# First layer of a DLRM tower as three fp32r passes on high and low halves

## The reference

```python
def _cin_layer(X0, Xi, W, b):
    Wr = W.reshape(H, F0_, Fi)
    return jnp.einsum('hjk,bjd,bkd->bhd', Wr, X0, Xi) + b[None, :, None]
e = jnp.stack([tbl_0[ids[:, 0]], ..., tbl_38[ids[:, 38]]], axis=1)   # (512, 39, 16)
Xi = e
for W, b in ((W0, b0), (W1, b1), (W2, b2)):                          # H = 128 each
    Xi = _cin_layer(e, Xi, W, b); res.append(Xi.sum(axis=2))
h = jnp.concatenate(res + [dense_ctx], axis=1)                       # (512, 400)
h = relu(h @ W_top1 + b_top1); h = relu(h @ W_top2 + b_top2); y = h @ W_top3
```

## Time and profile before

| | |
|---|---|
| median of 3 runs | 696.32 us (695.70 to 696.78) |
| the profiled execution | 697.1 us, its span 695.2 us |
| mean granted TensorE clock | 0.993 |
| TensorE busy | 651.2 us, 94% of the span |
| VectorE busy | 566.9 us, 82% |
| GpSimd busy | 444.2 us, 64% |
| ScalarE busy | 410.4 us, 59% |

### The profile page before, as it was taken

How to read it: one execution, slowest core, us unless ns; L and a number is a source line. 1 busy time by engine, 2 the same in 40 slices (tenths; PEclk the granted TensorE clock), 3 DMA queues, 4 the chain that set the end, 5 groups by cost and what they waited for, 6 DMA issues and landing times.

```text
span 695.2 us, 10601 instructions
## 1 busy us (share of the span) xinstructions
PE 651.2 (94%) x2856; PEld 495.7 (71%) x2856; DVE 566.9 (82%) x1495; ACT 410.4 (59%) x1369; POOL 444.2 (64%) x372
## 2 busy tenths in 40 slices
...
GB/s 214 49 128 232 151 60 122 6 124 6 124 7 105 24 3 88 43 64 68 58 75 42 83 7 37 95 28 103 18 114 17 99 16 18 111 1 6 0 2 1
DMA packets 39055, 44.33 MB, mean 64 GB/s; under 512 B 17427, under 2 KB 22253, under 8 KB 38867
## 3 DMA queue, kind: packets, MB, share of 16 engines
...
...
## 4 chain that ended last, share of the span: by engine, by line
PE 88%; POOL 4%; DVE 3%; DMA 2%; issue 2%; SPq 1%; ACT 1%; POOLq 0%; DVEq 0%
PE p_u L541 20%; PE p_u L542 20%; PE p_u L543 20%; PE p_x L518 13%; PE p_tower L560 5%; PE p_g L551 5%; POOL emb L257 3%; DVE parts L449 1%; DVE x2t L457 1%; PE p_tower L587 1%; PE p_tower L573 1%; DMA emb<-table_in,idx_all 1%; PE p_tower L572 1%; PE p_tower L579 1%; PE p_x L508 1%
## 5 line engine op out<-in xcount | busy, mean ns | idle before, releaser
L331 ACT ACTIVATE prod<-p_u,x0t 128x128 f32<-128x128 f32 x1024 | 290.9, 369 | 140.4 <-PE p_u L543 140.1
L449 DVE SCALAR_TENSOR_TENSOR parts<-p_u,x0t,parts 128x128 f32<-128x128 f32 x1024 | 283.7, 343 | 50.4 <-PE p_u L543 50.3
L541 PE MATMUL p_u<-w1h,x1h 128*128 128x512 f32 (+1 forms) x640 | 303.9, 475 | 4.1 <-DVE x1l L426 2.3
L542 PE MATMUL p_u<-w1l,x1h 128*128 128x512 f32 (+1 forms) x640 | 250.4, 391 | 0.0
L543 PE MATMUL p_u<-w1h,x1l 128*128 128x512 f32 (+1 forms) x640 | 250.2, 391 | 0.0
L273 POOL TENSOR_TENSOR parts<-parts,prod 128x512 f32<-128x512 f32 x128 | 173.1, 1353 | 77.6 <-ACT prod L331 66.3
L257 POOL DMA_INDIRECT emb<-table_in,idx_all x176 | 181.3, 1030 | 51.2 <-issue 47.8
L541 PEld LDWEIGHTS p_u<-w1h,x1h 128*128 128x128 f32 x640 | 120.9, 189 | 52.6 <-issue 20.4
L268 POOL TENSOR_TENSOR parts<-prod 128x512 f32<-128x512 f32 x64 | 89.6, 1400 | 99.6 <-ACT prod L331 99.3
L542 PEld LDWEIGHTS p_u<-w1l,x1h 128*128 128x128 f32 x640 | 121.5, 190 | 42.8 <-issue 20.2
L543 PEld LDWEIGHTS p_u<-w1h,x1l 128*128 128x128 f32 x640 | 120.7, 189 | 25.8
...
## 6 DMA issues: line engine op xcount, KB each, us to landing
...
bd<-x0t SPq DMA_DIRECT2D x128, 10.0 KB, 2.1
```

Source lines behind the costliest of these rows:

```text
L331: last = nc.scalar.activation(dst[:, i * H:(i + 1) * H], u[:, i * H:(i + 1) * H], ACT.Copy, scale=x0t[:, par, t, j:j + 1])
L449: nc.vector.scalar_tensor_tensor(out=chain[:, p, i, :], in0=u[:, i * H:(i + 1) * H], scalar=x0t[:, par, t, j:j + 1], in1=add, op0=ALU.mult ...
L541: nc.tensor.matmul(u, xh, wh, start=True, stop=False)
L542: nc.tensor.matmul(u, xh, wl, start=False, stop=False)
```

## The change

**What it does.** The first layer is computed as the second one already is. w0 and each z0 are split into a high half, rounded to fp32r, and the low half that is left. Instead of one float32 matmul a group, TensorE does three fp32r ones: high w by high z, low w by high z, high w by low z.

(In the diff, the hunks are in this order: constants, wait helper, GpSimd, ScalarE, VectorE, TensorE.) ScalarE makes each high half z0h one slot after the product. The low half z0l = z0 - z0h is made by VectorE two slots after the product for k = 0, 2, 4, 6, and by GpSimd for k = 1, 3, 5, in the tiles 0, 1 and 2 of the macro, between its first and second add. S_ADD moves one slot later, and with it x1f, x1h and x1l. The product no longer waits for TensorE to be done with the ring's place but for the low half made from it; the new rings z0h and z0l are the ones that wait for TensorE. w0 is split once at the start.

```diff
-S_ADD = [s + 6 for s in S_PAIR]
+S_HIGH = [s + 1 for s in S_PAIR]
+S_LOW = [s + 2 for s in S_PAIR]
+S_ADD = [s + 7 for s in S_PAIR]
+LOW_POOL = (1, 3, 5)
+LOW_DVE = (0, 2, 4, 6)
...
+        def wait_low(engine, M, k):
+            if M == 0:
+                engine.wait_ge(z0l_dve, k + 1)
+            elif k in LOW_DVE:
+                engine.wait_ge(z0l_dve, GROUPS + len(LOW_DVE) * (M - 1) + LOW_DVE.index(k) + 1)
+            else:
+                engine.wait_ge(z0l_pool, len(LOW_POOL) * (M - 1) + LOW_POOL.index(k) + 1)
...
+            def low_half(M, k):
+                rows = GROUP_ROWS[k]
+                pool.wait_ge(z0h_made, GROUPS * M + k + 1)
+                need(pool, l0_added, GROUPS * M + max(k - Z_RING + 1, 0))
+                nc.gpsimd.tensor_tensor(out=z0l[0:rows, k % Z_RING, :], in0=z0[0:rows, k % Z_RING, :],
+                                 in1=z0h[0:rows, k % Z_RING, :].bitcast(FP32), op=ALU.subtract).then_inc(z0l_pool, 1)
...
                     for i in (2, 3):
+                        if i == 2 and t < len(LOW_POOL) and (has_next or m < MACROS - 1):
+                            low_half(n * MACROS + m + 1, LOW_POOL[t])
...
+            def make_z0h(M, k):
+                rows = GROUP_ROWS[k]
+                act.wait_ge(z0_made, GROUPS * M + k + 1)
+                need(act, l0_added, GROUPS * M + max(k - Z_RING + 1, 0))
+                nc.scalar.activation(z0h[0:rows, k % Z_RING, :], z0[0:rows, k % Z_RING, :], ACT.Copy).then_inc(z0h_made, 1)
...
                 dve.wait_ge(b_in[k], 16 * (M + 1))
-                need(dve, l0_added, GROUPS * M + max(k - Z_RING + 1, 0))
+                if k >= Z_RING:
+                    wait_low(dve, M, k - Z_RING)
+                elif M > 0:
+                    wait_low(dve, M - 1, max(range(k, GROUPS, Z_RING)))
...
+                        for k in LOW_DVE:
+                            if prepares and s == S_LOW[k]:
+                                low_half(M + 1, k)
...
             for k in range(GROUPS):
                 product(0, 0, 0, k)
+                if k > 0:
+                    low_half(0, k - 1)
+            low_half(0, GROUPS - 1)
...
-                pe.wait_ge(z0_made, GROUPS * M + k + 1)
-                nc.tensor.matmul(p_x1[:], w0[0:rows, k * H:(k + 1) * H], z0[0:rows, k % Z_RING, :],
-                                 start=(k == 0), stop=(k == GROUPS - 1)).then_inc(l0_added, 1)
+                pe.wait_ge(z0h_made, GROUPS * M + k + 1)
+                wh, wl = w0h[0:rows, k * H:(k + 1) * H], w0l[0:rows, k * H:(k + 1) * H]
+                zh, zl = z0h[0:rows, k % Z_RING, :], z0l[0:rows, k % Z_RING, :]
+                nc.tensor.matmul(p_x1[:], wh, zh, start=(k == 0), stop=False)
+                nc.tensor.matmul(p_x1[:], wl, zh, start=False, stop=False)
+                wait_low(pe, M, k)
+                nc.tensor.matmul(p_x1[:], wh, zl, start=False, stop=(k == GROUPS - 1)).then_inc(l0_added, 1)
```

More of the change, by code:

```diff
@@ L87, in build @@
         w0 = sb("w0", [ROWS, GROUPS * H])
+        w0h = sb("w0h", [ROWS, GROUPS * H], FP32R)
+        w0l = sb("w0l", [ROWS, GROUPS * H], FP32R)
         w1h = sb("w1h", [H, F * H], FP32R)
@@ L104, in build @@
         z0 = sb("z0", [ROWS, Z_RING, COLS])
+        z0h = sb("z0h", [ROWS, Z_RING, COLS], FP32R)
+        z0l = sb("z0l", [ROWS, Z_RING, COLS], FP32R)
         x1f = sb("x1f", [H, COLS])
@@ L144, in build @@
         w0_summed = sem("w0_summed")
+        w0h_made = sem("w0h_made")
+        w0l_made = sem("w0l_made")
         w1h_made = sem("w1h_made")
@@ L154, in build @@
         z0_made = sem("z0_made")
+        z0h_made = sem("z0h_made")
+        z0l_dve = sem("z0l_dve")
+        z0l_pool = sem("z0l_pool")
         l0_added = sem("l0_added")
@@ L370, in body @@
                             evac_x0t(M + 1, n * (MACROS // 2) + (m + 1) // 2, (m + 1) % 2)
+                        for k in range(GROUPS):
+                            if prepares and s == S_HIGH[k]:
+                                make_z0h(M + 1, k)
                         if prepares and s == S_ADD[-1]:
@@ L399, in _ @@
             evac_x0t(0, 0, 0)
+            act.wait_ge(w0_summed, 1)
+            nc.scalar.activation(w0h[:], w0[:], ACT.Copy).then_inc(w0h_made, 1)
+            for k in range(GROUPS):
+                make_z0h(0, k)
             evac_x1(0)
@@ L418, in product, with low_half @@
                 dve.wait_ge(b_in[k], 16 * (M + 1))
-                need(dve, l0_added, GROUPS * M + max(k - Z_RING + 1, 0))
+                if k >= Z_RING:
+                    wait_low(dve, M, k - Z_RING)
+                elif M > 0:
+                    wait_low(dve, M - 1, max(range(k, GROUPS, Z_RING)))
                 nc.vector.tensor_tensor(out=z0[0:rows, k % Z_RING, :], in0=fac_b[0:rows, k, :], in1=fac_a[0:rows, par, :],
                                         op=ALU.mult).then_inc(z0_made, 1)
+            def low_half(M, k):
+                rows = GROUP_ROWS[k]
+                dve.wait_ge(z0h_made, GROUPS * M + k + 1)
+                need(dve, l0_added, GROUPS * M + max(k - Z_RING + 1, 0))
+                nc.vector.tensor_tensor(out=z0l[0:rows, k % Z_RING, :], in0=z0[0:rows, k % Z_RING, :],
+                                 in1=z0h[0:rows, k % Z_RING, :].bitcast(FP32), op=ALU.subtract).then_inc(z0l_dve, 1)
             def make_x1l(M, par):
```

4 lines of the change are left out of this document (3 added, 1 removed).

## The result

The changed kernel takes 742.5 us (median of 4 runs, 740.91 to 743.55) against 696.55 for the kernel before on the same chip. The ratio is 1.0658, with a 95% interval of 1.0641 to 1.0675: slower. The forecast was 728, with a range of 703 to 748. The profiled execution took 741.8 us, its span is 740.0, its mean clock 0.991.

What follows compares the result with a forecast made beforehand. TensorE was taken to set the pace, VectorE nearly as full. Plain macro: VectorE 34.57 + 2.4 + 1.3 + 0.3 = 38.57 us, +2.58; 12 times +31, tower 0, start +0.7: +31.7, forecast 728 us, range 703 to 748.

Steps and rivals of the forecast that it cites:

- VectorE becomes the bound, TensorE's saving is hidden: Plain macros: VectorE's work rises to 36.97 us, above TensorE's 34.9, so what TensorE saves doesn't show.
- TensorE's own saving: First layer's groups on TensorE: three passes save 0.16 us a group, 7 groups, 1.1 us a macro.
- 2.4 us for four low halves: VectorE in each macro: four added subtractions at 0.60 us each, 2.4 us.
- I take half, 1.3 us a macro: VectorE instructions beside GpSimd's adds: added collision loss between 0 and 2.6 us a macro, taken as 1.3.
- 0.3 us for x1h: End of a macro's preparation: VectorE waits 0 to 0.9 us for ScalarE's x1h, taken as 0.3.
- GpSimd stays under VectorE: GpSimd in a plain macro: 36 us with its low halves, full as well but below VectorE's load.
- I take nothing for these: Waits of fold_x2, TensorE and products 4 and 6 behind GpSimd's added work: covered by room, counted as 0.
- rival 3: GpSimd becomes the bound, 40 or 41 us a macro, TensorE's waits ending with its z0l: 745 to 755 us; 13%.
- Rival 2: Plain macros: VectorE's load alone, no further collisions, +1.0 to 1.2 us each: 707 to 711 us; 14%.
- rival 1: TensorE stays the bound, VectorE's load under 35.99 us, 15 x 1.1 = -17 us: 680 us; 7%.
- Tower macros 0: Three macros carrying the tower: TensorE's saving against VectorE's surplus, together -1 to +1.5 us, taken as 0.
- Start +0.7: First macro's preparation: z0h, low half and a pass in turn before x1f, +0.7 us, from 0 to 2.

Runs made afterwards that it cites:

- e6_fp32_pass: Changed kernel with all halves still made, but TensorE back to one float32 matmul on z0 a group; 746.16 us, ratio 1.0718 to the kernel before.
- e5_x1l_psum: Changed kernel with VectorE's x1l computed from the bank p_x1 instead of x1f, so one SBUF input; 729.8 us, ratio 1.0458 to the kernel before.
- e2_no_dve_low: Changed kernel without VectorE's four low halves from the second macro on, the high half streamed again instead; 729.76 us, ratio 1.0478 to the kernel before.
- e4_all_dve: Changed kernel with all seven low halves on VectorE and none on GpSimd; 741.06 us, ratio 1.0663 to the kernel before.
- e8_x1l_late: e5_x1l_psum with the high half three slots behind the product, VectorE's low half four, the passes eight; 723.4 us, ratio 1.0332 to the kernel before.
- e3_no_low: Changed kernel without any low half after the first macro, the high half streamed again instead; 713.8 us, ratio 1.0259 to the kernel before.
- e7_high_later: e3_no_low with the high half four slots behind the product instead of one, TensorE's groups one slot later; 692.26 us, ratio 0.992 to the kernel before.

## Why the prediction was right, point by point

- **VectorE becomes the bound, TensorE's saving is hidden.** The second half is right: e6_fp32_pass takes the saving away and the plain macro stays at 39.5. The first is right in part. VectorE is busy for all but 0.30 us of a plain macro, and e5_x1l_psum shortens it by what x1l gives back. But e2_no_dve_low takes 2.4 us of VectorE's work away and gains 0.9, and the page's chain has 40% GpSimd. The two share the loop. TensorE's own saving was put too high, 1.1 us a macro where e6_fp32_pass has 0.73; as it is hidden, this cost the forecast little. The 0.705 us for three passes measured 0.70. The remark that much of the float32 group's cost is the slow first pass behind it is right as arithmetic: in e6_fp32_pass that pass is back.
- **2.4 us for four low halves.** Right as VectorE's work: 0.60 from start to start at 348.14, and e4_all_dve adds three more that fit the sum. As a price it is less: the four are worth 0.9 us of the period (e2_no_dve_low).
- **Collisions, "I take half, 1.3 us a macro".** This is the term that was mis-sized. Four of the five places were right (products 4 and 6, low half 6, x1l; product 2 didn't collide), and VectorE lost at every one: 2.39 us above the 0.56 of before, where 2.6 was the upper end. e5_x1l_psum shows the largest as a price, 1.2 us a macro. The half stood for not knowing who comes second. The windows repeat to 0.02 us, so a loss is there in every macro or in none, and half is a hedge between two cases, not a case. The reason given was that ScalarE is held at each z0h. e8_x1l_late takes most of that wait away and products 4 and 6 lose as before, so for these two that reason doesn't hold; by the trace, GpSimd's own full program puts the adds there. With 2.4 in its place the plain macro comes to 39.7, against 39.50.
- **0.3 us for x1h.** The wait was 0; in its place VectorE waits 0.30 for TensorE before the last chain. The size came out by luck.
- **GpSimd stays under VectorE.** Right by its load: 32.6 us of work in 39.5. Wrong as "I take nothing for these": TensorE's waits for GpSimd's low halves are 18.0 us in the run beside 21.5 for VectorE's banks, which was the prediction's own sign for rival 3, and GpSimd leads the page's chain. Rival 3's time, 745 and up, was not reached. Rival 2, which ends at 707 to 711, fails on the collisions; rival 1 on VectorE's load.
- **Tower macros 0.** Wrong, +1.8 each, 5.3 us in all. e8_x1l_late has tower macros of 52.6 us against 54.1, so the order of the preparation matters there too; no run shows how the 1.8 us divide.
- **Start +0.7.** Measured 3.4, of which 1.9 is before the first transpose, with the gathers; the first transpose lies between 29.7 and 31.7 us in the traces of these kernels. The other 1.5 us lie in the preparation of the first macro, within the range of 0 to 2.
- **What the reasoning didn't have:** that the kernel is 1.47 us a macro longer with no low half at all (e3_no_low). It counted ScalarE's added 4.4 us as free because ScalarE had room. They bring a wait at each of them, with the scalings behind it; with the high halves and the groups later (e7_high_later) 1.9 us are gone. With the low halves in, the same move gave 0.45 (e8_x1l_late).
- **How the 13 us between the forecast's +31.7 and the measured 44.8 divide:** the plain stretches have 36.1 (with the 2.3 at the end) for 31, the tower macros 5.3 for 0, the start 3.4 for 0.7. So the time lies in the range by terms that were each too low, and by a bound that is shared.
